# Other orders of the stages on each engine, in the lead, the first batch and the middle batches of a Macaron block

## The reference

```python
x = x + 0.5 * ffn(layernorm(x))     # "a"
x = x + attention(layernorm(x))     # "att"
x = x + 0.5 * ffn(layernorm(x))     # "c"

# ffn: hidden size 512, gelu; per batch the weights get a rank-one-like addition,
# built from products of even and odd tokens 1..16 of that batch:
h   = gelu(x @ (W1 + scale*m1).T + b1);  out = h @ (W2 + scale*m2).T + b2
# attention: 16 heads of 64, q and k are RMS-normalized per head
gate   = softplus(k . u_n / 8)                       # per key and head
scores = q.k/8 - (i-j) * omega_eff * gate[j], causal; y = softmax(scores) @ v; y @ Wproj
```

## Time and profile before

| | |
|---|---|
| median of 3 runs | 797.78 us |
| profiled execution | 796.84 us, span 794.8 us |
| PE busy | 765.8 us, 96% |
| DVE, ACT, POOL busy | 84%, 83%, 81% |
| lead, up to the first stage of "first" on PE | 0 to 75.1 us |
| "first" | 75.1 to 159.0 us |
| one body | 92.7 to 93.2 us |
| "final" | 716.3 us to the end |

### The profile page before, as it was taken

How to read it: one execution, slowest core, us unless ns; L and a number is a source line. 1 busy time by engine, 2 the same in 40 slices (tenths; PEclk the granted TensorE clock), 3 DMA queues, 4 the chain that set the end, 5 groups by cost and what they waited for, 6 DMA issues and landing times.

```text
span 794.8 us, 25588 instructions
## 1 busy us (share of the span) xinstructions
PE 765.8 (96%) x9669; PEld 549.4 (69%) x9669; DVE 667.6 (84%) x1874; ACT 655.8 (83%) x1420; POOL 641.5 (81%) x751
## 2 busy tenths in 40 slices
...
GB/s 191 13 162 42 134 44 141 62 135 97 29 161 69 149 68 73 144 78 154 29 132 72 126 105 28 162 68 148 70 68 149 69 162 29 122 83 151 87 48 27
DMA packets 97297, 77.12 MB, mean 97 GB/s; under 512 B 71662, under 2 KB 84080, under 8 KB 97176
## 3 DMA queue, kind: packets, MB, share of 16 engines
...
...
## 4 chain that ended last, share of the span: by engine, by line
PE 84%; ACT 4%; issue 3%; DVE 3%; DMA 2%; POOL 2%; SPq 1%; POOLq 0%; ACTq 0%; DVEq 0%
PE ps L1048 15%; PE ps L1049 14%; PE ps L1050 14%; PE ps L1197 8%; PE ps L1170 8%; PE ps L1198 8%; PE ps L1152 6%; PE ps L1199 3%; PE ps L1172 2%; DMA qk<-qkn 2%; PE ps L1065 1%; PE ps L1179 1%; ACT qkn L934 1%; PE ps L1075 1%; ACT sq L933 1%
## 5 line engine op out<-in xcount | busy, mean ns | idle before, releaser
L813 POOL TENSOR_TENSOR pt_l<-pt 128x512 f16<-128x512 f32 x368 | 320.3, 900 | 70.0 <-ACT pt L1008 69.8
L1008 ACT ACTIVATE pt<-ps 128x512 f32<-128x512 f32 (+1 forms) x384 | 175.1, 530 | 29.3 <-PE ps L1199 17.1
L839 POOL TENSOR_TENSOR qkn<-qkn,rs 128x512 f32<-128x512 f32 x128 | 130.5, 1048 | 30.9 <-ACT rs L945 30.9
L1197 PE MATMUL ps<-qk 128*128 128x512 f16 (+3 forms) x512 | 146.9, 300 | 0.0
L1198 PE MATMUL ps<-qk 128*128 128x512 f16 (+3 forms) x512 | 146.5, 299 | 0.0
L1508 DVE CUSTOM_DVE_ANT_0 masked<-ps,causal_row 128x512 f16<-128x512 f32 x224 | 130.4, 619 | 18.0 <-PE ps L1170 15.7
L1048 PE MATMUL ps<-v_buf,pt 128*128 128x65 f16 x1280 | 129.8, 194 | 0.9 <-POOL pt_l L813 0.8
L1049 PE MATMUL ps<-v_buf,pt 128*128 128x65 f16 x1280 | 129.8, 193 | 0.0
L1050 PE MATMUL ps<-v_buf,pt_l 128*128 128x65 f16 x1280 | 129.5, 193 | 0.0
L1048 PEld LDWEIGHTS ps<-v_buf,pt 128*128 128x128 bf16 x1280 | 118.0, 98 | 6.6 <-issue 1.2
L1049 PEld LDWEIGHTS ps<-v_buf,pt 128*128 128x128 bf16 x1280 | 117.5, 98 | 3.2
...
## 6 DMA issues: line engine op xcount, KB each, us to landing
...
qk<-gtt SPq DMA_DIRECT2D x64, 8.0 KB
qk<-nmt SPq DMA_DIRECT2D x64, 2.0 KB
y_hl<-ytt SPq DMA_TRANSPOSE x63, 3.1
```

The source lines that it names most:

```text
L813: g.tensor_tensor(pt_l[:, h % 2, c], pt[:, h % 2, c], pt_h[:, h % 2, c], ALU.subtract).then_inc(s_pt_l, 1)
L839: g.tensor_tensor(qk, qk, r.unsqueeze(4).broadcast_to([P, 2, 2, 2, D]), ALU.mult).then_inc(s_qkn, 1)
L1008: a.activation(pt[:, h % 2, c], ps[:, j, 0:width], ACT.Exp).then_inc(s_exp, 1)
L1197: pe.matmul(dst, k1(h)[:, keys], q1(h)[:, kb * P:T], start=True, stop=False)
```

## The change

The stages, their instructions, their tiles and their number stay the same. Only the lists "lead", "first" and "body" of the five engines are other permutations; the same stages stand in each part. Since banks of the ring are given out in PE's order, the banks of the stages change too. "final" and the code of all stages are unchanged. In words, for the parts that the next sections speak of:

- PE, lead: of the three `warm` stages one of 8 matmuls goes to the very start, one of 10 between `m` and `h`, the one of 6 behind `out`; before, they stood behind `m` (6), behind `qk 1 3` (8) and behind `gl 0` (10). `setup` comes ahead of `zt a`. `v 0 0` goes between `qk 1 0` and `qk 1 1`, `v 0 1` ahead of `gl 0`, `v 0 2` ahead of `t 3`.
- ACT, lead: `sel` ahead of `ln1 a`; `v 0 0` ahead of `qkn 0 0`.
- DVE, lead: `us` behind `ln2 a`; `b2` ahead of `setup`; `uu` behind `h`.
- POOL, lead: `m` ahead of `clear` and `ul`.
- first and body: the same kind of exchange all through the lists. In the body `v 0 3` moves from the middle of the maxima to the end; `s 12`, `s 13` go ahead of `a 1`, `a 2`; POOL takes `yt 6` ahead of `pl 15`; SP takes `add c` later.

The diff, cut to the lead and to the end of the body ("first" has changes of the same kind):

```diff
     "tensor": {
         "lead": [
-            ("zt", "a", NEXT), ("setup", NEXT), ("m", "a", NEXT), ("warm", 0, 6, NEXT), ("h", "a", NEXT),
-            ("out", "a", NEXT), ("uu", NEXT), ("zt", "att", NEXT), ("qk", 0, 0, NEXT), ("qk", 0, 1, NEXT),
-            ("qk", 0, 2, NEXT), ("qk", 0, 3, NEXT), ("qk", 1, 0, NEXT), ("qk", 1, 1, NEXT), ("qk", 1, 2, NEXT),
-            ("qk", 1, 3, NEXT), ("warm", 1, 8, NEXT), ("t", 0, NEXT), ("t", 1, NEXT), ("v", 0, 0, NEXT),
-            ("gl", 0, NEXT), ("warm", 1, 10, NEXT), ("v", 0, 1, NEXT), ("gr", 0, NEXT), ("t", 2, NEXT),
+            ("warm", 1, 8, NEXT), ("setup", NEXT), ("zt", "a", NEXT), ("m", "a", NEXT), ("warm", 1, 10, NEXT),
+            ("h", "a", NEXT), ("out", "a", NEXT), ("warm", 0, 6, NEXT), ("uu", NEXT), ("zt", "att", NEXT),
+            ("qk", 0, 0, NEXT), ("qk", 0, 1, NEXT), ("qk", 0, 2, NEXT), ("qk", 0, 3, NEXT), ("qk", 1, 0, NEXT),
+            ("v", 0, 0, NEXT), ("qk", 1, 1, NEXT), ("qk", 1, 2, NEXT), ("qk", 1, 3, NEXT), ("t", 0, NEXT),
+            ("t", 1, NEXT), ("v", 0, 1, NEXT), ("gl", 0, NEXT), ("t", 2, NEXT), ("gr", 0, NEXT), ("v", 0, 2, NEXT),
             ("t", 3, NEXT), ("a", 0, NEXT), ("a", 1, NEXT), ("qk", 2, 0, NEXT), ("qk", 2, 1, NEXT), ("a", 2, NEXT),
-            ("a", 3, NEXT), ("qk", 2, 2, NEXT), ("a", 4, NEXT), ("nm", 0, NEXT), ("qk", 2, 3, NEXT),
-            ("v", 0, 2, NEXT), ("v", 0, 3, NEXT), ("qk", 3, 0, NEXT), ("qk", 3, 1, NEXT), ("qk", 3, 2, NEXT),
-            ("a", 5, NEXT), ("s", 0, NEXT), ("a", 6, NEXT), ("qk", 3, 3, NEXT), ("s", 1, NEXT), ("a", 7, NEXT),
-            ("t", 4, NEXT), ("gl", 1, NEXT), ("nm", 1, NEXT), ("pv", 0, NEXT), ("t", 5, NEXT), ("v", 1, 0, NEXT),
-            ("t", 6, NEXT),
+            ("a", 3, NEXT), ("qk", 2, 2, NEXT), ("qk", 2, 3, NEXT), ("a", 4, NEXT), ("nm", 0, NEXT), ("a", 5, NEXT),
+            ("qk", 3, 0, NEXT), ("qk", 3, 1, NEXT), ("qk", 3, 2, NEXT), ("a", 6, NEXT), ("s", 0, NEXT),
+            ("a", 7, NEXT), ("v", 0, 3, NEXT), ("qk", 3, 3, NEXT), ("t", 4, NEXT), ("s", 1, NEXT), ("nm", 1, NEXT),
+            ("t", 5, NEXT), ("gl", 1, NEXT), ("v", 1, 0, NEXT), ("pv", 0, NEXT), ("t", 6, NEXT),
         ],
...
         "body": [
...
-            ("pv", 10, THIS), ("t", 1, NEXT), ("wp", 1, THIS), ("t", 2, NEXT), ("gr", 0, NEXT), ("s", 12, THIS),
-            ("t", 3, NEXT), ("h", "c", LAST), ("pv", 11, THIS), ("a", 0, NEXT), ("s", 13, THIS), ("a", 1, NEXT),
-            ("v", 0, 3, NEXT), ("qk", 2, 0, NEXT), ("qk", 2, 1, NEXT), ("a", 2, NEXT), ("pv", 12, THIS),
-            ("a", 3, NEXT), ("qk", 2, 2, NEXT), ("qk", 2, 3, NEXT), ("s", 14, THIS), ("a", 4, NEXT),
-            ("out", "c", LAST), ("qk", 3, 0, NEXT), ("a", 5, NEXT), ("pv", 13, THIS), ("qk", 3, 1, NEXT),
-            ("qk", 3, 2, NEXT), ("qk", 3, 3, NEXT), ("nm", 0, NEXT), ("s", 15, THIS), ("a", 6, NEXT),
-            ("pv", 14, THIS), ("gl", 1, NEXT), ("a", 7, NEXT), ("t", 4, NEXT), ("wp", 2, THIS), ("nm", 1, NEXT),
-            ("t", 5, NEXT), ("t", 6, NEXT),
...
+            ("v", 0, 2, NEXT), ("pv", 10, THIS), ("gr", 0, NEXT), ("wp", 1, THIS), ("t", 2, NEXT), ("t", 3, NEXT),
+            ("h", "c", LAST), ("pv", 11, THIS), ("a", 0, NEXT), ("s", 12, THIS), ("a", 1, NEXT), ("qk", 2, 0, NEXT),
+            ("qk", 2, 1, NEXT), ("s", 13, THIS), ("a", 2, NEXT), ("qk", 2, 2, NEXT), ("qk", 2, 3, NEXT),
+            ("a", 3, NEXT), ("pv", 12, THIS), ("a", 4, NEXT), ("qk", 3, 0, NEXT), ("qk", 3, 1, NEXT),
+            ("qk", 3, 2, NEXT), ("out", "c", LAST), ("qk", 3, 3, NEXT), ("a", 5, NEXT), ("pv", 13, THIS),
+            ("a", 6, NEXT), ("s", 14, THIS), ("t", 4, NEXT), ("nm", 0, NEXT), ("gl", 1, NEXT), ("s", 15, THIS),
+            ("a", 7, NEXT), ("wp", 2, THIS), ("t", 5, NEXT), ("nm", 1, NEXT), ("pv", 14, THIS), ("t", 6, NEXT),
+            ("v", 0, 3, NEXT),
         ],
...
     "scalar": {
         "lead": [
-            ("ln1", "a", NEXT), ("sel", NEXT), ("setup", NEXT), ("wq", 0, NEXT), ("zt", "a", NEXT),
-            ("qk", 0, 2, NEXT), ("qk", 0, 3, NEXT), ("qkn", 0, 0, NEXT), ("qk", 1, 0, NEXT), ("qkn", 0, 1, NEXT),
-            ("qk", 1, 1, NEXT), ("qk", 1, 2, NEXT), ("qk", 1, 3, NEXT), ("qkn", 1, 0, NEXT), ("qkn", 1, 1, NEXT),
-            ("t", 0, NEXT), ("t", 1, NEXT), ("v", 0, 0, NEXT), ("gate", 0, NEXT), ("rows", 0, NEXT),
...
+            ("sel", NEXT), ("ln1", "a", NEXT), ("wq", 0, NEXT), ("zt", "a", NEXT), ("setup", NEXT),
+            ("qk", 0, 2, NEXT), ("qk", 0, 3, NEXT), ("v", 0, 0, NEXT), ("qkn", 0, 0, NEXT), ("qk", 1, 0, NEXT),
+            ("qkn", 0, 1, NEXT), ("qk", 1, 1, NEXT), ("qk", 1, 2, NEXT), ("qk", 1, 3, NEXT), ("qkn", 1, 0, NEXT),
+            ("qkn", 1, 1, NEXT), ("t", 0, NEXT), ("t", 1, NEXT), ("v", 0, 1, NEXT), ("gate", 0, NEXT),
+            ("rows", 0, NEXT), ("t", 2, NEXT), ("v", 0, 2, NEXT), ("t", 3, NEXT), ("rows", 1, NEXT),
...
     "vector": {
         "lead": [
-            ("ln1", "a", NEXT), ("us", NEXT), ("ln2", "a", NEXT), ("zl", NEXT), ("uu", NEXT), ("setup", NEXT),
-            ("zt", "a", NEXT), ("m", "a", NEXT), ("b2", NEXT), ("h", "a", NEXT), ("add", "a", NEXT),
...
+            ("ln1", "a", NEXT), ("ln2", "a", NEXT), ("us", NEXT), ("zl", NEXT), ("b2", NEXT), ("setup", NEXT),
+            ("zt", "a", NEXT), ("m", "a", NEXT), ("h", "a", NEXT), ("uu", NEXT), ("add", "a", NEXT),
...
     "gpsimd": {
         "lead": [
-            ("ul", NEXT), ("clear", NEXT), ("m", "a", NEXT), ("ud", NEXT), ("wvl", NEXT), ("wol", NEXT),
+            ("m", "a", NEXT), ("clear", NEXT), ("ul", NEXT), ("ud", NEXT), ("wvl", NEXT), ("wol", NEXT),
             ("qkn", 0, 0, NEXT), ("qkn", 0, 1, NEXT), ("qkn", 1, 0, NEXT), ("qkn", 1, 1, NEXT), ("gate", 0, NEXT),
-            ("qkn", 2, 0, NEXT), ("qkn", 2, 1, NEXT), ("pl", 0, NEXT), ("qkn", 3, 0, NEXT), ("qkn", 3, 1, NEXT),
+            ("qkn", 2, 0, NEXT), ("qkn", 2, 1, NEXT), ("qkn", 3, 0, NEXT), ("pl", 0, NEXT), ("qkn", 3, 1, NEXT),
             ("gate", 1, NEXT),
         ],
...
         "body": [
...
-            ("pl", 10, THIS), ("qkn", 0, 1, NEXT), ("qkn", 1, 0, NEXT), ("qkn", 1, 1, NEXT), ("gate", 0, NEXT),
-            ("m", "c", LAST), ("pl", 11, THIS), ("pl", 12, THIS), ("h", "c", LAST), ("pl", 13, THIS),
-            ("yt", 4, THIS), ("yt", 5, THIS), ("qkn", 2, 0, NEXT), ("pl", 14, THIS), ("qkn", 2, 1, NEXT),
-            ("qkn", 3, 0, NEXT), ("qkn", 3, 1, NEXT), ("pl", 15, THIS), ("yt", 6, THIS), ("gate", 1, NEXT),
...
+            ("qkn", 0, 1, NEXT), ("pl", 10, THIS), ("qkn", 1, 0, NEXT), ("gate", 0, NEXT), ("qkn", 1, 1, NEXT),
+            ("m", "c", LAST), ("pl", 11, THIS), ("h", "c", LAST), ("pl", 12, THIS), ("qkn", 2, 0, NEXT),
+            ("yt", 4, THIS), ("yt", 5, THIS), ("pl", 13, THIS), ("qkn", 2, 1, NEXT), ("qkn", 3, 0, NEXT),
+            ("pl", 14, THIS), ("qkn", 3, 1, NEXT), ("yt", 6, THIS), ("pl", 15, THIS), ("gate", 1, NEXT),
         ],
...
         "body": [
             ("ln1", "a", NEXT), ("yt", 7, LAST), ("rows", 2, THIS), ("yt", 0, THIS), ("yt", 1, THIS),
             ("rows", 3, THIS), ("nm", 2, THIS), ("yt", 2, THIS), ("yt", 3, THIS), ("nm", 3, THIS), ("rows", 0, NEXT),
-            ("rows", 1, NEXT), ("add", "c", LAST), ("yt", 4, THIS), ("yt", 5, THIS), ("nm", 0, NEXT),
-            ("nm", 1, NEXT), ("yt", 6, THIS),
+            ("rows", 1, NEXT), ("yt", 4, THIS), ("yt", 5, THIS), ("nm", 0, NEXT), ("add", "c", LAST),
+            ("yt", 6, THIS), ("nm", 1, NEXT),
         ],
```

More of the change, by code:

```diff
@@ L110 @@
+            ("s", 1, NEXT), ("t", 6, NEXT),
         ],
         "first": [
-            ("s", 2, THIS), ("t", 7, THIS), ("ln1", "a", NEXT), ("s", 3, THIS), ("v", 1, 1, THIS),
-            ("ln2", "a", NEXT), ("yt", 0, THIS), ("s", 4, THIS), ("zt", "a", NEXT), ("yt", 1, THIS), ("s", 5, THIS),
-            ("v", 1, 2, THIS), ("m", "a", NEXT), ("s", 6, THIS), ("h", "a", NEXT), ("nm", 2, THIS), ("yt", 2, THIS),
-            ("v", 1, 3, THIS), ("s", 7, THIS), ("ln1", "att", NEXT), ("ln2", "att", NEXT), ("zt", "att", NEXT),
@@ new lines @@
+            ("s", 3, THIS), ("yt", 0, THIS), ("ln2", "a", NEXT), ("s", 4, THIS), ("zt", "a", NEXT), ("yt", 1, THIS),
+            ("s", 5, THIS), ("m", "a", NEXT), ("h", "a", NEXT), ("t", 7, THIS), ("s", 6, THIS), ("ln1", "att", NEXT),
+            ("ln2", "att", NEXT), ("zt", "att", NEXT), ("yt", 2, THIS), ("s", 7, THIS), ("qk", 0, 0, NEXT),
+            ("qk", 0, 1, NEXT), ("qk", 0, 2, NEXT), ("nm", 2, THIS), ("qk", 0, 3, NEXT), ("qkn", 0, 0, NEXT),
+            ("qk", 1, 0, NEXT), ("v", 0, 0, NEXT), ("qk", 1, 1, NEXT), ("qk", 1, 2, NEXT), ("qkn", 0, 1, NEXT),
@@ new lines @@
+            ("v", 1, 3, THIS), ("h", "a", NEXT), ("ln1", "c", LAST), ("s", 6, THIS), ("nm", 2, THIS),
+            ("ln2", "c", LAST), ("s", 7, THIS), ("ln1", "att", NEXT), ("zt", "c", LAST), ("ln2", "att", NEXT),
+            ("yt", 2, THIS), ("zt", "att", NEXT), ("s", 8, THIS), ("yt", 3, THIS), ("qk", 0, 0, NEXT),
+            ("s", 9, THIS), ("qk", 0, 1, NEXT), ("qk", 0, 2, NEXT), ("qk", 0, 3, NEXT), ("qkn", 0, 0, NEXT),
```

(18 more changed lines are left out.)

185 lines of the change are left out of this document (90 added, 95 removed).

## The result

The changed kernel took 815.08 us (median of 4 runs, 814.02 to 816.72) beside 798.26 us of before (now four runs): ratio 1.0209, 95% interval 1.0193 to 1.0225. It is slower by 2.1%, far outside the noise, where 794.2 us was forecast.

What follows compares the result with a forecast made beforehand. PE, busy 96% of the span, was taken as the floor. Lead -1.9, "first" -0.5 and six bodies -1.2 sum to -3.6 us: span 791.2, execution 793.2, against the median 794.2 us; range 789.0 to 801.0.

Steps and rivals of the forecast that it cites:

- F: Six bodies: bank waits at `a 2` and likely `wp 2` go, POOL just in time; -0.2 us each, -1.2 for six.
- R1: Rival, slower: POOL is late at the end of every body, so `pv 15` and the next body wait; 801.4 us, chance 0.20.
- R2: Rival, no change: the lead's clock falls before `t 0` and stays low, bodies and "first" as before; 798.1 us, chance 0.20.
- R3: Rival, more gain: all port and clock gains come and bodies win 0.6 us each; 789.4 us, chance 0.10.
- A: Lead up to the end of `out a`: reorders along DVE's chain sum to -0.7 us, bounds +1.0 and -1.6.
- B: Lead, from `out a` to the first `t`: clock holds and ACT's four blocks go closer together; -0.4 us.
- C: Lead, from `t` to `a 0`: PE idles longer before `t 0` and its clock falls; +0.4 us.
- D: Lead, from `a 0` to its end: `v 0 2` moves out and part of a slow clock phase goes; -1.2 us.
- E: "first": same work, some waits of 0.2 to 1.1 us exchanged for others; -0.5 us, bounds +2 and -2.

Runs made afterwards that it cites:

- e4: Changed kernel with the `pt_l` subtractions of `pl 6` and `pl 7` in the six bodies made 4 columns wide: 796.95 us, 0.9973 of before.
- e6: Changed kernel with every `shift` computed as four one-column tensor_scalar instructions in place of one scalar_tensor_tensor: 800.77 us, 1.0019 of before.
- e5: Changed kernel with the `pt_l` subtractions of `pl 8` and `pl 9` in the six bodies made 4 columns wide: 814.12 us, 1.0186 of before.
- e2: Kernel before with the changed lists of "lead" and "first" alone, "body" as before: 798.30 us, 0.9992 of before.

## Why the prediction was wrong, point by point

- **F, the bodies (-0.2 each forecast, +2.95 measured), is the step that failed.** I counted POOL's room at `pv 15` and two bank waits. `pv 15` indeed had no wait, and the one at `a 2` went. But I did not lay the banks' readers against the new PE order. The way on PE from the last matmul of `out a` to `zt att` shrank from 6.05 us (before) to 4.72 (e4, same order as the changed kernel, without the wait), a step that was never in the sum. And DVE's `shift` of c was taken at its length in the old trace. Moving GpSimd's work beside it made it 2.55 for 0.72. e4 and e6 show that the second is the cause of most of it: with the short way left as it is, the bodies are 92.7 in e4 and 93.4 to 94.0 in e6. That the short way turns DVE's lateness into a wait of PE is my reading: no run puts the way alone back cleanly, and in e6 0.51 us of wait are left.
- The bounds of F (up to +6) fell short for the same reason: they were POOL's. I had no term for the clock in a body, worth 1.6 us in four of six.
- **R1** (POOL late at the body's end, 801.4) was on the right side with the wrong mechanism: no wait at `pv 15`, and e5, which frees POOL of two `pl`, gave nothing back. **R2** fits the lead and first batch: e2 gives no change. **R3** is out.
- **A (-0.7; +0.85 measured at the add).** z_a at 7.20 as forecast; om_e 0.17 for 0.94 and the gate factors 0.24 for 1.53, so the term that I could not tell came out at its good end, -1.2. The trace agrees with the rule quoted from the Trainium skill ("SBUF — State Buffer", on the shared port pair): an instruction with two SBUF inputs is not blocked by memsets. What I left out is the COPY two lines on, held for 2.79 us. The same section counts a copy among the instructions that can run in a two-port mode, and such a one is blocked by any GpSimd instruction.
- **B, C, D:** `t 0` at 38.85 for 38.77, `a 0` at 50.52 for 49.34, first matmul of "first" at 75.55 for 75.1. Less what came before, B gave -0.8 (forecast -0.4), C cost +1.1 (+0.4) and D gave -0.7 (-1.2). The granted clock fell to 0.50 in 39.6 to 43.0 us, as I said. POOL's first `qkn` came at 34.10, not near 32.9, since A was late. The lead is +0.5 where -1.9 was summed.
- **E ("first", -0.5; -0.4 measured)** came out in size; no run tests why.
- Both signs of being wrong that I named came: bodies off by over 0.5 us each, and a longer lead.
